# Attention scores as half-array products over the head pair's own tiles, issued in bursts of two steps

## The reference

```
for each of 8 batches, for each of 16 heads (width 64):
    Q1,Q2 = halves of xn @ Wq + bq ;  K1,K2 = halves of xn @ Wk + bk ;  V = xn @ Wv + bv
    P = softmax(Q1 K1' / 8) - lam * softmax(Q2 K2' / 8)          # 512 x 512 each
    O = P V
attention = 0.2 * (layernorm(concat(O) @ Wo + bo) * gamma + beta)
experts   = top-1 of 8 experts: gelu(xn @ w1[e] + b1[e]) @ w2[e] + b2[e], times the route's probability
result    = x + attention + experts
```

## Time and profile before

| | |
|---|---|
| Median of 3 runs | 1818.81 us (1817.0 to 1823.01) |
| Profiled execution | 1818.79 us |
| Its span, first to last instruction | 1817.0 us |
| TensorE, weight loads | busy 98%, 76% |
| VectorE, ScalarE, GpSimd | busy 85%, 78%, 35% |
| Attention steps | 26.6 to about 1453 us of the span |
| Experts and output | from about 1455 us |

### The profile page before, as it was taken

The page is one execution under the profiler, slowest core; times in us unless marked ns, Lnnn a source line. Parts: engine busy times, 40 slices in busy tenths (PEclk is TensorE's granted clock), DMA queues, the critical chain, the costliest instruction groups (busy, mean ns, idle before and its releaser), DMA issues. The chain is left out here.

```text
span 1817.0 us, 32461 instructions
## 1 busy us (share of the span) xinstructions
PE 1782.6 (98%) x10494; PEld 1389.1 (76%) x10494; DVE 1544.9 (85%) x2636; ACT 1415.0 (78%) x3364; POOL 638.4 (35%) x711
## 2 busy tenths in 40 slices
PE   6999999999999999999999999999999999999998
PEld 5777777777777777777777777777767789999998
DVE  4988988899889888988898889888999866887677
ACT  5988888888888888888888888888888776676632
POOL 2443222222222222222222322222226555553265
PEclk8999999999999999999999999999999999999999
DMA  8989988888888888888888888888887667667797
GB/s 248 238 247 258 246 226 218 222 235 220 218 225 239 220 220 229 239 221 218 231 231 223 219 231 235 221 218 224 224 209 198 192 246 261 236 241 249 273 370 301
DMA packets 196277, 427.79 MB, mean 235 GB/s; under 512 B 27824, under 2 KB 91312, under 8 KB 188048
## 3 DMA queue, kind: packets, MB, share of 16 engines
q1 hardware_dynamic: 191264, 411.72, 80.6%
q0 software_dynamic: 4688, 13.51, 2.2%
q10 hardware_dynamic: 160, 0.52, 0.1%
HBM read 175.17 MB, written 49.15 MB: 123 GB/s over the span
## 5 line engine op out<-in xcount | busy, mean ns | idle before, releaser
L614 ACT ACTIVATE e<-p_score,nmax 128x512 f32<-128x512 f32 x1024 | 697.1, 688 | 139.0 <-DVE nmax L961 137.6
L961 DVE TENSOR_REDUCE nmax<-p_score 128x2 f32<-128x1024 f32 x512 | 622.9, 1217 | 150.6 <-PE p_score L1111 146.6
L480 POOL TENSOR_SCALAR e<-e,rrec,lam 128x512 f32<-128x512 f32 x512 | 394.1, 770 | 978.7 <-DVE rrec L928 978.2
L1111 PE MATMUL p_score<-ks,qs 128*128 128x512 f32 x2048 | 581.3, 406 | 7.8 <-DMA ks<-k_parts 5.0
L1111 PEld LDWEIGHTS p_score<-ks,qs 128*128 128x128 f32 x2048 | 366.5, 189 | 178.1 <-issue 60.8
L1074 PE MATMUL p_proj<-xh,w 128*128 128x512 f32 x1024 | 384.7, 417 | 5.9 <-DVE k_parts L903 4.5
L935 DVE SCALAR_TENSOR_TENSOR pm<-e,rrec 128x512 f32<-128x512 f32 x512 | 383.3, 749 | 0.4 <-POOL e L480 0.2
L566 ACT COPY pT<-p_tr 128x512 f32<-128x512 f32 x512 | 301.7, 589 | 99.1 <-PE p_tr L1123 98.8
L1123 PEld LDWEIGHTS p_tr<-consts,pm 128*128 128x128 f32 x2048 | 249.6, 140 | 79.9 <-issue 19.8
L1123 PE MATMUL p_tr<-consts,pm 128*128 128x128 f32 x2048 | 308.9, 273 | 1.4 <-ACT pT L566 1.2
L1140 PE MATMUL p_pv<-pT,v 128*64 128x512 f32 x1024 | 247.7, 605 | 0.7 <-ACT pT L566 0.7
(11 more groups left out here) (215 smaller groups left out, 1850.9 us busy)
## 6 DMA issues: line engine op xcount, KB each, us to landing
ks<-k_parts SPq DMA_DIRECT2D x510, 256.0 KB, 4.9
qs<-q_parts SPq DMA_DIRECT2D x512, 128.0 KB, 4.6
w<-weight_parts_scratch SPq DMA_DIRECT2D x56, 1024.0 KB, 10.5
w<-in_w SPq DMA_DIRECT2D x46, 1024.0 KB, 7.2
oT_parts_scratch<-oT SPq DMA_DIRECT2D x32, 512.0 KB, 6.4
op<-oT_parts_scratch SPq DMA_DIRECT2D x16, 1024.0 KB, 9.2
wv<-weight_parts_scratch SPq DMA_DIRECT2D x56, 256.0 KB, 5.5
weight_parts_scratch<-w SPq DMA_DIRECT2D x8, 1024.0 KB, 5.4
```

The costliest lines, as they stand in the source:

```text
L480: nc.gpsimd.tensor_scalar(e2, e2, rrec[:, g % 4, 1:2], lam[:, 0:1], ALU.mult, ALU.mult).then_inc(s_e2, 1)
L614: nc.scalar.activation(ex[:, g % EX, m, :], p_score[g % 2][:, m, :], ACT.Exp, bias=nmax[:, g % 2, m:m + 1], accum_out=rsum[:, g % 4, m:m + ...
L961: vec.tensor_reduce(nmax[:, g % 2, :], p_score[g % 2][:, :, :], AXX, ALU.max, negate=True).then_inc(s_max, 1)
L1111: last_op = nc.tensor.matmul(p_score[g % 2][:, m, :], qs[j][u][:, m, qt * P:(qt + 1) * P], ks[j][u][:, m, part, :], start=(part == 0), sto ...
```

## The change

- **Scores.** `qs`, `ks` and their DMAs go. `scores` reads `parts` directly: map m lies in rows 64m to 64m+63, so a product is 64 rows x 128 columns, and maps 0 and 1 use the two row halves of the array. Three part products are made per map (`TERMS`), alternating between the maps: six products a step where there were four. `parts` is doubled (one set for even, one for odd pairs); `high_part` waits for the scores that read the set two pairs before.
- **Bursts.** All three loops go two steps at a time (`BURST`). TensorE: scores g and g+1, transposes g-2, input transposes (at step 0), routing, projections (q0 and k0 at step 0, q1 at 4, k1 at 6), values (at step 2), transposes g-1, then `times_v` of the pair before: key tile 0 at step 2, 1 at step 4, 2 and 3 at step 6, or 0 and 1 at step 4 and 2 and 3 at step 6 where its bank is in use.
- **ScalarE:** `copy_pT(g-3)`, high part of k0 (at step 2), input high part, `copy_o`, `copy_pT(g-2)`, the exponentials of g and of g+1, high part of q0, q1 or k1 (at step 0, 4, 6), weight splitting.
- **VectorE:** maximum g, combine g-1, maximum g+1, low part of k0 (step 2), input low part, `low_o`, reciprocals g, `add_bv`, small jobs of step g, reciprocals g+1, combine g, small jobs of g+1, low part of q0, q1 or k1 (steps 0, 4, 6).

The core of the diff:

```diff
-        parts = {"q": [sb(f"q_parts{u}", [P, 2, S], F32R) for u in range(2)],
-                 "k": [sb(f"k_parts{u}", [P, 2, S], F32R) for u in range(2)]}
-        qs = [[sb(f"qs{j}{u}", [P, 2, S], F32R) for u in range(2)] for j in range(2)]
-        ks = [[sb(f"ks{j}{u}", [P, 2, 2, S], F32R) for u in range(2)] for j in range(2)]
+        parts = [{x: [sb(f"{x}_parts{j}{u}", [P, 2, S], F32R) for u in range(2)] for x in "qk"} for j in range(2)]
...
+        TERMS = ((0, 0), (0, 1), (1, 0))
+        PROJECTED = {0: ("q0", "k0"), 4: ("q1",), 6: ("k1",)}
+        FIRST_HALF = {0: "q0", 4: "q1", 6: "k1"}
+        SECOND_HALF = {2: "k0"}
+        V_STEP = 2
+        PV_AT, PV_LATE = {2: (0,), 4: (1,), 6: (2, 3)}, {4: (0, 1), 6: (2, 3)}
...
+            for g in range(0, STEPS, BURST):
+                pair, st = g // TPP, g % TPP
+                if g >= 2 * BURST:
+                    copy_pT(g - BURST - 1)
+                if st in SECOND_HALF and pair + 1 < NPAIRS:
+                    high_part(pair + 1, SECOND_HALF[st])
+                if st == BURST and group_at(pair):
+                    x_high(group_at(pair))
+                if st == 0 and pair >= 2:
+                    copy_o(pair - 2)
+                if g >= BURST:
+                    copy_pT(g - BURST)
+                exponentials(g)
+                exponentials(g + 1)
+                if st in FIRST_HALF and pair + 1 < NPAIRS:
+                    high_part(pair + 1, FIRST_HALF[st])
...
+            for g in range(0, STEPS, BURST):
+                pair, st = g // TPP, g % TPP
+                maximum(g)
+                if g >= BURST:
+                    combine(g - 1)
+                maximum(g + 1)
+                if st in SECOND_HALF and pair + 1 < NPAIRS:
+                    low_part(pair + 1, SECOND_HALF[st])
...
+                reciprocals(g)
...
+                if st == V_STEP and pair + 1 < NPAIRS:
+                    add_bv(pair + 1)
+                beside(g)
+                reciprocals(g + 1)
+                combine(g)
+                beside(g + 1)
+                if st in FIRST_HALF and pair + 1 < NPAIRS:
+                    low_part(pair + 1, FIRST_HALF[st])
...
             def scores(g):
...
                 if qt == 0:
-                    pe.wait_ge(s_dup[j][u], 16 * DUPS * (pair // 2 + 1))
+                    pe.wait_ge(s_lo, 4 * pair + 2 * u + 2)
                 if g >= 2:
                     pe.wait_ge(s_exp, 2 * g - 2)
-                for m in range(2):
-                    for part in range(2):
-                        last_op = nc.tensor.matmul(p_score[g % 2][:, m, :],
-                                                   qs[j][u][:, m, qt * P:(qt + 1) * P], ks[j][u][:, m, part, :],
-                                                   start=(part == 0), stop=(part == 1))
+                for i, (a, b) in enumerate(TERMS):
+                    for m in range(2):
+                        rows = slice(m * D, (m + 1) * D)
+                        last_op = nc.tensor.matmul(p_score[g % 2][:, m, :], q[rows, a, qt * P:(qt + 1) * P],
+                                                   k[rows, b, :], start=(i == 0), stop=(i == 2))
...
+            for g in range(0, STEPS, BURST):
                 pair, st = g // TPP, g % TPP
                 scores(g)
-                if g >= LAG:
-                    transposes(g - LAG)
+                scores(g + 1)
+                if g >= BURST:
+                    transposes(g - BURST)
...
+                for what in PROJECTED.get(st, ()):
+                    if pair + 1 < NPAIRS:
+                        project(pair + 1, what)
...
+                if g >= BURST:
+                    transposes(g - 1)
+                bank_in_use = pair + 1 < NPAIRS and with_logits(pair + 1) or group_at(pair)
+                key_tiles = (PV_LATE if bank_in_use else PV_AT).get(st)
+                if pair >= 1 and key_tiles:
+                    times_v(pair - 1, key_tiles)
```

More of the change, by code:

```diff
@@ L551, in high_part @@
                 act.wait_ge(s_proj, n + 1)
[L552 to L553 removed]
+                if pair >= 2:
+                    act.wait_ge(s_score, TPP * (pair - 2) + QT * (u + 1))
                 if n == 0:
@@ L556, in high_part @@
                 b = bias[:, pair % PAIRS, bias_of[what[0]] + u:bias_of[what[0]] + u + 1]
-                nc.scalar.activation(parts[what[0]][u][:, 0, :], bank_of(pair, what)[:, :],
+                nc.scalar.activation(parts[j][what[0]][u][:, 0, :], bank_of(pair, what)[:, :],
                                      ACT.Identity, bias=b).then_inc(s_hi, 1)
@@ L597, in _, with exponentials @@
             high_qk(1, 1)
[L599 to L607, removed]
-                if g >= LAG:
-                    copy_pT(g - LAG)
+            def exponentials(g):
                 for m in range(2):
@@ L616, in _, with split_weights @@
                                          accum_out=rsum[:, g % 4, m:m + 1]).then_inc(s_exp, 1)
[L617 to L620, removed]
+            def split_weights(pair, st):
+                if pair == 0 and st == 3:
                     high_v(2)
@@ L955, in _, with maximum @@
             route_on = routing()
[L956 to L959, removed]
+            def maximum(g):
                 dve.wait_ge(s_score, g + 1)
@@ L962, in _, with beside @@
                                   negate=True).then_inc(s_max, 1)
[L963 to L979, removed]
+            def beside(g):
+                nonlocal moments_on
+                pair, st = g // TPP, g % TPP
+                if st >= TPP - BURST and pair + 1 < NPAIRS and group_at(pair + 1):
+                    normalise(group_at(pair + 1), st - (TPP - BURST))
+                later_step = g % (TPP * PAIRS) - (TPP * X_PAIRS[0] - BURST - LATER_STEPS)
                 if batch_of(pair) + 1 < B and 0 <= later_step < LATER_STEPS:
@@ L997, in _ @@
                     next(route_on)
+            for g in range(0, STEPS, BURST):
+                pair, st = g // TPP, g % TPP
+                maximum(g)
[4 more added lines that the diff above has]
+                    low_part(pair + 1, SECOND_HALF[st])
+                if st == BURST and group_at(pair):
+                    x_low(group_at(pair))
+                if st == 0 and pair >= 2 and not whole(pair - 2):
+                    low_o(pair - 2)
+                reciprocals(g)
+                if g == 0:
+                    dve.wait_ge(s_bv, 32)
+                    add_bv(0)
+                if st == V_STEP and pair + 1 < NPAIRS:
[6 more added lines that the diff above has]
+                    low_part(pair + 1, FIRST_HALF[st])
             assert next(route_on, "over") == "over"
-            for g in range(STEPS - 2, STEPS):
-                reciprocals(g)
-            combine(STEPS - 2)
             combine(STEPS - 1)
@@ L1119, in transposes @@
                     pe.wait_ge(s_v, 1)
-                if g >= 1:
+                else:
                     pe.wait_ge(s_pT, g)
@@ L1192, in _ @@
                     values(pair + 1)
-                if st == X_STEP and group_at(pair):
-                    transpose_x(group_at(pair))
-            transposes(STEPS - 4)
-            times_v(NPAIRS - 2, (0, 1))
-            transposes(STEPS - 3)
-            times_v(NPAIRS - 2, (2, 3))
+                if g >= BURST:
[4 more added lines that the diff above has]
+                    times_v(pair - 1, key_tiles)
             transposes(STEPS - 2)
```

62 lines of the change are left out of this document (19 added, 43 removed).

## The result

The changed kernel takes 1927.3 us (median of 4, 1924.7 to 1929.4) against 1819.5 us before: ratio 1.059, 95% interval 1.057 to 1.061. It is 108 us slower where +57 was forecast: the sign, the range (1850 to 1930) and the mechanism held, the size was nearly double.

The account below looks back on a forecast made before the run. TensorE's order bounds the old kernel; after the change a VectorE-ScalarE loop does. 63 pairs x 22.86 us, 15.7 for the last and 27 of small jobs put the last reciprocals +57.6 us later: 1876 us, range 1850 to 1930.

Parts of the forecast that it names:

- TensorE's products: Score products on TensorE: two row halves run together, 0.70 us a step instead of 0.93, 1.87 us less per pair of heads.
- its sum: TensorE's work per pair of heads after the change, mode changes included: 21.5 us.
- rival 2: Weight loads not hidden under products of the same rows: TensorE 23.6 to 25.7 us a pair, 1900 to 2035 us; chance 0.10.
- rivals 2 and 3: The second: rival 2. The third: row halves do not run together, 1.40 us a step, about 2125 us; chance 0.05.
- The ring: Closed VectorE-ScalarE loop from reciprocals through combinations, maxima, exponentials and back: 5.88 us, setting 22.86 us a pair of heads.
- rival 1: TensorE keeps setting the pace and the change gains: 21.6 us a pair, about 1771 us; chance 0.13.
- The copy ahead of the exponentials: ScalarE's copy of the first transposed tile: its path takes 5.03 us per burst, inside the loop, so hidden.
- the loop after step 2: VectorE-ScalarE loop in the burst after step 2 of a pair, with no low part in it: 5.22 us.
- GpSimd's multiplication: GpSimd's 0.77 us multiplication, needed before combine g+1, which comes 2.5 us after the reciprocals: covered.
- The small jobs: Normalisations, statistics and the like on the loop: about 2.1 us a batch; with input parts, routing, weight splitting 27 us.
- Input parts: Input low parts on VectorE behind k0's low part: 14 x 0.3 = 4 us.
- The start: First exponential waits only for the table load, 23.75 us instead of 27.9: -4.1 us; step 1's reciprocals at about 26.6.

Follow-up runs that it names:

- e1: Changed kernel with the fourth part product (low q times low k) added back, eight half-array products per step: 1931.4 us (1.061).
- e10: Changed kernel with four full-array products per step in place of the six, scores not the reference's: 1926.5 us (1.059).
- e2: Changed kernel with high parts of q0, q1, k1 between the two exponentials and their low parts behind reciprocals g: 1859.2 us (1.022).
- e6: Changed kernel with e2 and e5 together, plus combine g and small jobs of g+1 ahead of reciprocals g+1: 1829.7 us (1.005).
- e8: e6 with the low part of k0 ahead of reciprocals g again: 1823.6 us (1.002).
- e7: Changed kernel with the copy of the first transposed tile between the exponentials of g and g+1, not ahead of both: 1995.9 us (1.097).
- e5: Changed kernel with reciprocals g directly behind the second maximum, ahead of the low parts of k0 and input and low_o: 1908.2 us (1.049).
- e4: Changed kernel with combine g-1 behind both maxima instead of between them: 1965.4 us (1.080).
- e3: Kernel before, in its old step order, with only the new half-array scores and doubled parts, no qs, ks or their DMAs: 1837.9 us (1.010).

## Why the prediction was right in kind and short in size

**TensorE's products: right; its sum somewhat high.** Halves run together: a burst's twelve products take 1.66 us and six take 0.96, so three pairs of products need 0.70, 0.233 each, the value taken.

```profile
908.97 1.66 PE L1099 MATMUL p_score<-k_parts,q_parts 64*128 64x512 f32 x12
...
919.67 0.96 PE L1099 MATMUL p_score<-k_parts,q_parts 64*128 64x512 f32 x6 [0.26 <-ACT e L568]
```

With that rivals 2 and 3 are out, and so is the rule of the Trainium skill ("TensorE: Matmul & The Clock Gate", Part 3, The mechanism) that was weighed against the change: the loads of the next pair go to rows in use and cost nothing visible. The sum, with eleven mode changes at 2.3 us a pair of heads, was 21.5 where the smallest distances add up to 20.9 at most, so it was some 0.6 us too high. It did not matter here, as e1 and e10 show.

**The ring: right, and it is the cause.** e2, e6 and e8 remove its links and the time goes; e1 and e10 change the work beside it and the time stays. With that rival 1, by which TensorE would set the pace, is out too. Its 1771 us were not reached even with the ring gone: e8 is at 1824, for a reason that stays open.

**The copy ahead of the exponentials: hidden, as said.** e7 shows more: it has to stand there.

**What was mis-sized.** The last reciprocals came at 1560.2 us, forecast 1511. The 49 us are:

- The ring in a plain pair of heads: 23.26 us, not 22.86, 63 x 0.40 = 25 us. The step "reciprocals 0.07" is 0.11 when the combination follows it, other distances are 0.01 to 0.03 longer, and the loop after step 2 is 5.37, not 5.22: there I had called GpSimd's multiplication covered. That was worked out for combine g+1 alone. Combine g also waits for it, and reciprocals g stand behind k0's low part.
- The small jobs, with what the last pair has beside its ring: 63 pairs take 1511.0 us, 45.6 above 63 x 23.26, and the last pair's three bursts 20.4 instead of 15.7. That is 50 us instead of 28.5, so 22. Input parts were taken as 0.3 us per pair, but the burst that has them takes 6.10 us where a plain one takes 5.37, so 14 x 0.43 = 6. The cause is the same omission, and e5, which removes it, gives back 14 x 0.86 = 12 us in these pairs. The other jobs beside the steps are 3.2 us a batch, not 2.1: 8 more in seven batches. Most of the rest lies in the last batch, where one maximum of the last pair waits 2.94 us for scores.
- The start: the first exponential begins at 23.76 us as forecast (23.8), but the second reciprocals only at 28.76, not 26.6, behind `add_bv(0)`: 2.

The distance from forecast to measured time is 51 us, as 1927.3 is the median and 1924.7 the profiled execution. That the result is still inside the range of 1850 to 1930 is partly luck: the upper end was set for the cheap end of rival 2, which didn't happen, and the forecast's own range ended at 1905.

The forecast of TensorE at 90 to 95% was met with 94%; "reciprocals of odd steps idle about 1 us" with 1.1 to 1.4 (0.2 after step 2, in plain pairs).

## What to carry to other kernels

Relieving an engine that is full can gain nothing: before a change that groups steps, write down for each engine which instruction waits for another engine and what is queued behind it, and follow the ring until it closes; its length over the steps in it is the pace, however idle the engines look. Put work that waits for nobody into the gap and nothing between the last wait and the next instruction that another engine needs. Busy shares don't find the ring, and 98% on TensorE doesn't rule it out. An instruction that is done for both steps of a burst (here GpSimd's multiplication) must be checked for each of them, in the burst where its own input is latest. And when a ring is cut, look for the next longer one first: e4 and e7 each closed another.

## What the runs showed of the hardware that I had not expected

GpSimd's multiplication takes 0.77 us before and in e8, but 1.00 in the mean in the changed kernel (page, 512 of them: 511.9 us against 394.1), 1.25 where it starts beside a combination. The combination beside a running multiplication takes 1.20 instead of 0.74. Beside a maximum, which reads PSUM, neither is slowed: in e8 the multiplication at 957.94 us, beside the maximum of 957.76, takes 0.77.

```profile
957.76 1.21 DVE L934 TENSOR_REDUCE nmax<-p_score 128x2 f32<-128x1024 f32 x1
957.94 0.77 POOL L446 TENSOR_SCALAR e<-e,rrec,lam 128x512 f32<-128x512 f32 x1 [1.26 <-DVE rrec L903]
```

The Trainium skill has this rule in "SBUF — State Buffer", Who interferes with whom: a VectorE instruction with two SBUF inputs, as the combination is, contends with a GpSimd instruction that reads SBUF, one with at most one SBUF input, as the maximum is, doesn't. The trace agrees on both, with 1.25 against 0.77 us for GpSimd. The prediction did not use it.

A mode change of the array costs little when a burst shares it. Done every step, as in e3, it costs an estimated 0.28 us in and out, more than a third of the 0.70 us of products that it serves.
